# Linear attention: where VectorE scales one head's queries, and where ScalarE copies them

## The reference, cut to what matters

```python
q, k, v = x @ Wq, x @ Wk, x @ Wv
beta = sigmoid(x @ Wb + bb);  gate = silu(x @ Wg)
q = silu(causal_dwconv(q, qconv_w, qconv_b))   # 4 taps per channel
k = silu(causal_dwconv(k, kconv_w, kconv_b))
q = layernorm(q, qn_w, qn_b);  k = layernorm(k, kn_w, kn_b)   # per head
for t: S = (1 - b_t) * S + b_t * v_t k_t^T;  o_t = S q_t
y = (o * gate) @ Wo
```

## Time and profile before

| | |
|---|---|
| median of 3 runs | 1059.94 us (1059.01 to 1061.52) |
| the profiled execution | 1060.79 us |
| its span, first to last instruction | 1059.0 us |
| mean granted TensorE clock | 0.985 |
| busy: PE, DVE, ACT, POOL | 95%, 73%, 64%, 51% |
| the loop of steps 2 to 15 | 445.9 to 734.7 us |

### The profile page before, as it was taken

One profiled execution on the slowest core, in us unless ns is written; L12 is line 12 of the kernel. 1 busy time (PEld: TensorE's weight loads), 2 busy tenths in 40 slices (PEclk: granted clock), 3 DMA queues, 4 the chain that ended last, 5 costly groups with the idle time before them and its releaser, 6 DMA issues.

```text
span 1059.0 us, 19066 instructions
## 1 busy us (share of the span) xinstructions
PE 1008.1 (95%) x6781; PEld 795.1 (75%) x6781; DVE 769.0 (73%) x1567; ACT 679.6 (64%) x1244; POOL 541.1 (51%) x454
## 2 busy tenths in 40 slices
PE   7999999999999998699999999999899999999997
PEld 4333333467888896598988989899799788888997
DVE  5889999646766845899998999899766465344843
ACT  4588888766554347888887888888645353333454
POOL 3351310114069551889888898898315001447543
PEclk9999999999999999899999999999999999999999
DMA  4443443223224201543244233421311124555100
GB/s 98 88 78 58 77 68 58 61 88 94 80 88 134 39 1 34 197 145 106 96 154 142 106 105 135 150 105 66 125 32 41 46 61 104 155 149 167 61 21 21
DMA packets 83626, 96.21 MB, mean 91 GB/s; under 512 B 29912, under 2 KB 68524, under 8 KB 81484
## 3 DMA queue, kind: packets, MB, share of 16 engines
q1 hardware_dynamic: 82800, 94.05, 31.4%
q10 hardware_dynamic: 732, 0.95, 0.3%
HBM read 82.29 MB, written 1.41 MB: 79 GB/s over the span
## 4 chain that ended last, share of the span: by engine, by line
PE 54%; DVE 11%; POOL 4%; ACT 4%; issue 3%; DVEq 2%; DMA 1%; POOLq 0%; ACTq 0%
PE late_bank L65 7%; PE late_bank L67 7%; PE late_bank L66 7%; PE lin_pair L65 3%; PE lin_pair L67 3%; PE lin_pair L66 3%; PE lin_pair L1863 3%; DVE lin_conv_k L2250 2%; PE gold_bank L65 2%; PE gold_bank L67 2%; PE gold_bank L66 2%; PE lin_pair L1960 2%; DVE gold_part L1476 2%; PE lin_pair L1949 2%; DVE lin_conv_q L2250 2%
## 5 line engine op out<-in xcount | busy, mean ns | idle before, releaser
L744 ACT ACTIVATE attn_probs<-attn_rows_k 128x512 f32<-128x512 f32 x256 | 138.9, 595 | 24.4 <-PE attn_rows_k L590 21.2
L590 PE MATMUL attn_rows_k<-attn_q_stack,attn_k_stack 50*128 50x512 f32 x256 | 94.0, 446 | 0.0
L3063 DVE TENSOR_TENSOR late_mids<-late_mids,late_bank 128x512 f32<-128x512 f32 (+1 forms) x50 | 34.3, 687 | 77.8 <-PE late_bank L67 74.8
L855 DVE TENSOR_REDUCE attn_row_max<-s_sum 128x1 f32<-128x1024 f32 x62 | 75.6, 1220 | 10.9 <-PE attn_rows_q L574 5.0
L603 PE MATMUL attn_ctx<-attn_probs,attn_v 128*32 128x256 f32 x1024 | 81.5, 391 | 1.5
L855 DVE TENSOR_REDUCE attn_row_max<-attn_rows_q 128x1 f32<-128x1024 f32 x62 | 75.9, 1224 | 8.9 <-PE attn_rows_q L574 5.4
L65 PE MATMUL late_bank<-net_x_part_low,late_w_T 128*128 128x512 f32 (+1 forms) x192 | 77.9, 405 | 0.0
L66 PE MATMUL late_bank<-net_x_part_low,late_w_T 128*128 128x512 f32 (+1 forms) x192 | 76.1, 396 | 0.0
L67 PE MATMUL late_bank<-net_x_part_low,late_w_T 128*128 128x512 f32 (+1 forms) x192 | 76.1, 396 | 0.0
L3163 POOL TENSOR_TENSOR late_mids<-late_mids,late_raw_w_T_last 128x512 f32<-128x512 f32 x22 | 29.5, 1363 | 90.2 <-DMA late_raw_w_T_last<-top_weights 90.2
L1611 POOL TENSOR_TENSOR gold_mids<-gold_mids,s_later 128x512 f32<-128x512 f32 x32 | 51.9, 1660 | 45.5 <-DMA s_later<-gold_weights 45.5
(11 more groups left out here) (478 smaller groups left out, 3551.1 us busy)
## 6 DMA issues: line engine op xcount, KB each, us to landing
s_raw_w_o<-query_norms SPq DMA_DIRECT2D x16, 1024.0 KB, 4.8
lin_mix<-decay_sums SPq DMA_DIRECT2D x16, 512.0 KB, 6.0
lin_q_dec<-decay_sums SPq DMA_DIRECT2D x16, 512.0 KB, 7.2
s_later<-gold_weights SPq DMA_DIRECT2D x16, 256.0 KB, 3.6
attn_k_stack<-s_part SPq DMA_DIRECT2D x30, 128.0 KB, 3.5
s_raw_ring<-in_L_ffn_Wg SPq DMA_DIRECT2D x12, 256.0 KB, 2.8
s_raw_ring<-in_L_ffn_Wu SPq DMA_DIRECT2D x12, 256.0 KB, 3.1
attn_k_stack<-s_part SPq DMA_DIRECT2D x33, 64.0 KB, 2.3
```

What stands on the lines that cost most here:

```text
L590: pe.matmul(out, k_stack[rows, h % SLOTS, t * P:(t + 1) * P], q_stack[rows, h % SLOTS, :], start=True, stop=True).then_inc(scored_k, 1)
L744: act.activation(probs[:, (2 * k + odd) % PB, side * HALF:(side + 1) * HALF], ring_bank(("exped", 4 * k + n + 1)), ACT.Exp).then_inc(exped, 1)
L855: dve.tensor_reduce(row_max[h % 2][:, tile:tile + 1], ps_tile[tile_bank(n)][:, :], axis=AX, op=ALU.max)\
```

## The change

In VectorE's step the product `scale_q(n-1)` moves behind the keys' convolution. In ScalarE's step `silu_k(n)` and `copy_v(n)` move ahead of `q_transposed(n-1)`. Nothing is added or left out; the work and the tiles are the same.

```diff
@@ LinearAttention.act, loop over n
                 high_gate(n - 1)
             if live(n):
                 silu_q(n)
+                silu_k(n)
+                copy_v(n)
             if live(n - 1):
                 q_transposed(n - 1)
-            if live(n):
-                silu_k(n)
-                copy_v(n)
@@ LinearAttention.dve, loop over n
             if live(n):
                 convolve(n, 0, 3, self.q_tapped, self.q_conved)
+                convolve(n, 1, 1, self.k_tapped, self.k_conved)
                 scale_q(n - 1)
-                convolve(n, 1, 1, self.k_tapped, self.k_conved)
```

## The result

| | before | with the change |
|---|---|---|
| median (4 runs each) | 1059.47 us (1058.04 to 1061.52) | 1093.53 us (1090.29 to 1096.84) |
| the profiled execution | 1060.79 us | 1096.84 us |
| its span | 1059.0 us | 1095.1 us |
| mean granted TensorE clock | 0.985 | 0.979 |

The changed kernel is slower: ratio 1.0297, 95% interval 1.0261 to 1.0333. The forecast was 1100 (1076 to 1114).

A forecast was written before the change was run, and what follows sets the result against it. TensorE was taken to bound the loop. The terms 33.9 - 2 - 8.3 + 17 gave +40.6 us on the profiled 1060.79, so 1101.4, or 1100 us against the median; range 1076 to 1114.

The forecast's parts named there:

- The place and the mechanism: In the loop, VectorE's moved product waits until GpSimd's second `rows_k` product ends, ending at 609.97 in step 9.
- 2.42 us a step: `rows_k` starts 2.42 us later in each of the fourteen steps 2 to 15, 33.9 us in all.
- 8.3 us won: TensorE's waits in the loop, the largest ahead of `turn_k`, are all won back: 8.3 us.
- 2 us off for a step with late means: In one step like step 7, GpSimd's first product still runs when VectorE asks and ends sooner: 2 us off.
- Falls of the clock, ten for 17 us: Gaps in the loop make TensorE's clock fall in ten of fourteen steps, 1.7 us each: 17 us, bounds 0 and 24.
- ScalarE at nothing: In the loop, ScalarE's later copy of the queries stays hidden with 2 us to spare; costed at nothing.

The follow-up runs named there:

- the kernel with half a product: The whole change, but GpSimd's second product of `rows_k` covers only 4 of the 8 chunks from head 1 on; 1070.00 us, ratio 1.0078.
- the early tap: The whole change, and ScalarE puts the keys' fourth tap between chunks 6 and 7 of the normalisation of k; 1066.75 us, ratio 1.0047.

## Why the prediction was right, and what was mis-sized

- *The place and the mechanism.* Right, and shown by experiments: the product stands for GpSimd's second product (it takes 1.2 us where GpSimd is made to wait for it), to that one's end (half of it, 1.10 us less), and because both of its own inputs lie in SBUF (with one in PSUM it does not stand). Offsets from ScalarE's second tap of q came out within 0.1 us of the working: the convolution ended 8.70 after it, GpSimd's second product began at 8.27, VectorE's product ended at 11.74. One sentence of the working is too narrow: that the contention is between GpSimd and a VectorE instruction with two tiles of SBUF. The kernel before has a VectorE instruction with one that stands as well (last section).
- *2.42 us a step.* Step by step the same: a clean step was 20.79 and is 23.17, 2.38 more. The gap reads 2.26, since it is counted from the end of `turn_k`, and without a gap `rows_k` starts 0.15 us ahead of that end (608.82 against 607.93 + 1.04).
- *8.3 us won.* Right in kind: no gap of more than 0.2 us is left ahead of `turn_k`.
- *2 us off for a step with late means.* Wrong in sign. In step 7 GpSimd was late, but by so little that its second product still began 0.11 us before VectorE asked; it then also ended later, and the product took 3.35 us. The effect exists: in the kernel with half a product GpSimd was 0.6 us later still in one step, and there VectorE's product took 1.39.
- *Falls of the clock, ten for 17 us.* Mis-sized: five, for 5 x 1.6 = 8 us, so that the sum was 9 us too high by this term alone. In 5 of 14 steps with gaps of 2.04 to 2.50 us there were falls; three rows with two falls between them were too few to tell 0.35 from 0.67, and leaning on the likeness with one of them was wrong. The Trainium skill's limit ("TensorE: Matmul & The Clock Gate", section "Why this matters for your kernels"), no idle gaps over about 3 us, would give none; here five came, so neither it nor my ten is right.
- *ScalarE at nothing.* Right for the whole change, with one thing left unsaid: without ScalarE's half, VectorE's half would have cost some 31 us more.
- *The sum by its terms* for the profiled pair: 14 gaps and the won time 33.9 - 8.3 = 25.6 forecast, 2.36 + 13 x 23.17 - 278.40 = 25.2 measured; late means -2 forecast, nothing or slightly more than nothing measured; falls 17 forecast, 8 measured; 2.45 us arose before the loop, where nothing is changed, and 0.5 behind it. So the forecast for the pair, 40.6 against 36.05, is closer than its largest mistake: the 9 us too many for the clock were partly made up by 2 us taken off wrongly and by some 3 us that the prediction knows nothing of. That much of the closeness is luck.

The runs of the changed kernel spread over 6.5 us, with granted clocks from 0.979 (1096.84 us) to 0.985 (1090.29): 0.006 of 1093 us is 6.6 us, so the number of falls could account for the spread. Only one of the four has a trace, so this is not shown.

## What to carry to other kernels

Before an instruction is moved on VectorE, look at what GpSimd is doing at the new place: where both read tiles of SBUF, as a product of two tiles does on VectorE, the later one stood in these runs until the earlier was through, and the record shows it as a longer duration and not as a wait. A cover that hides one wait (here 8.3 us in the loop) can put the instruction beside a longer neighbour. Where both must run at about the same time, fix the order by a signal that comes just after the first engine has asked (here the end of the instruction ahead of it, which let GpSimd start 0.16 us after VectorE), so that the second already stands ready and need not be woken; the same order without it depended on 0.1 us.

## What the runs showed of the hardware

- Who is first is sharp: asking 0.05 us after GpSimd's start cost the full 2.2 us, asking 0.08 ahead of it nothing.
- VectorE's product ended 1.07 to 1.09 us after GpSimd's instruction, in seven kernels, against 1.21 alone.
- One SBUF input can be enough. In step 9 of the kernel before, the instruction that adds a constant to the variances (one tile of SBUF, 8 elements a partition) took 0.57 us and ended at 611.63, 0.03 after GpSimd's scaling of the values (609.68, 1.92). In step 10 no instruction of GpSimd ran beside it, and it took 0.17. The long ones, eight with that of step 1, all began within a long GpSimd instruction and ended 0.02 to 0.03 us after it. Which VectorE instructions with one SBUF input stand, and why, no run here tested.

```profile
611.06 0.57 DVE L2272 TENSOR_SCALAR lin_var_eps_q<-lin_mean_var_q 128x8 f32<-128x8 f32 x1
632.32 0.17 DVE L2272 TENSOR_SCALAR lin_var_eps_q<-lin_mean_var_q 128x8 f32<-128x8 f32 x1
```

- Falls of TensorE's clock by the gap between `turn_k` and `rows_k`: none at 0.4 to 1.5 us (three kernels), 5 of 14 at 2.04 to 2.50 (the changed kernel), three of three at 2.06 to 2.30 (the early tap), about one per step at 3.04 to 3.37 (only VectorE's half). Ahead of `turn_k` there was one after 1.83 us in the kernel before and one after 1.70 with only ScalarE's half. In the changed kernel four of the five came in every second step (532, 580, 628, 676 us). What decides within the same gap stays open.
